# Dense experts of a small mixture layer: gating the outputs of plain tokens instead of gating the inputs

## The chip, the cores and the metric
The kernel runs on 1 core of one Trainium2 chip. The metric is the device time of one execution in microseconds (us), the median of several. All engines of the core take part: TensorE (PE, its weight loads shown as PEld), VectorE (DVE), ScalarE (ACT), GpSimd (POOL) and the DMA queues (SP, POOL).

## What is computed
Two layers over 4 batches of 1024 tokens with 128 features: a mamba mixer with an MLP, a first mixture of experts with residual and norms, attention with relative positions, and a second mixture with capacity. The change touches the first mixture alone:

```
gate_scores = softmax(x @ Wg.T + bg)
topk_scores, topk_idx = top_k(gate_scores, 2)
expert_outputs = einsum('bsd,eod->bseo', x, W) + b      # 8 experts, 128 -> 128
selected = take_along_axis(expert_outputs, topk_idx[..., None], axis=2)
output = sum(selected * topk_scores[..., None], axis=2)
```

All 8 experts are computed for all tokens; the gates of the 6 that were not chosen are zero.

## The kernel before, in words
Everything is float32 unless a line says bf16. A float32 product runs as two passes, so each matmul of the program is two matmul and two weight-load instructions in the trace.

**Slots.** The first layer is a pipeline over batches, written out by hand: `SLOTS` (L74) lists for each slot which batch is in the mixer (m), which in MLP and experts (p) and which in the tail, the norms, queries, keys and values before the attention (q). Slots 1, 2 and 3 have all of the work of the experts beside a mixer; slot 4 has (p = 3, q = 2) and no mixer; attention comes after slot 5. Each engine runs its own program in order, and they meet through semaphores.

**The loop over chunks.** In a slot the mixer goes through 8 chunks of 128 tokens, c = 0 to 7 (PE at L882, DVE at L2096, ACT at L1347). In each chunk PE does the product with the carried state (`chunk_carried`, L665), the new state (`chunk_state`, L657), transposes (`chunk_front`, L635), the decay sums (`chunk_after`, L650) and the output (`chunk_out`, L675). DVE does `chunk_carry` (L1884), `chunk_scaled` (L1901), `chunk_inputs` (L1875, L1878), `chunk_weights` (L1890, which waits for ACT's exponential, L1278), and after each second chunk `gate` (L1913, L1916). `chunk_out` of chunk c waits for `chunk_scaled` of c, and DVE's next chunk waits for PE's new state. At c = 7 PE runs `mix_out(m, 0)`; after the loop `mix_out(m, 1)`, which waits for the last `gate` and for ACT's squares (L1295). DVE closes the slot with `mix_norm` (L1930), two halves.

**The experts in that loop.** Tokens, turned so that features are on partitions, lie in `xnT` (128 x 1024). At c = 1 PE computes the logits (`route0`), at c = 2 and 3 DVE finds the two best and builds the gates `gsel` (128 tokens x 8 tiles x 8 experts). `gate_parts` (L1965) then cuts the gates into three bf16 parts `g3` (L1972 to L1977). At c = 4 PE turns `gsel` (8 transposes, L787) and `g3` (8 transposes, L791), ACT copies `gT` (L1262), DVE copies `g3T` (L1981). Then come 16 steps k, for each half H of the tokens and each expert e: `gate_rows` (L795) spreads the gate of expert e over 128 partitions by a bf16 product with `pick_rows`, DVE multiplies it with the tokens into `xs` (128x512, L1991), and `expert_sum` (L807) adds four 128x128 products with `w_exp` into one PSUM bank. Each half begins with the biases, four products of `gT` with `b_exp`, and ends with `expert_added` (L1993): one add into `x2` and the statistics of the norm (L1759, L1764). `SUMS_AT` and `SUMS_LAST` (L79) say at which chunk each step is issued: 0 to 2 at c = 4, 3 to 6 at c = 5, 7 to 10 at c = 6, 11 and 12 at c = 7, and 13 to 15 after `mix_out(m, 1)`. `keep_clock` (L596) issues bf16 products whose results nobody reads.

**Slot 4.** Without a mixer the steps are interleaved with the first products of attention: `score_pair` on PE and the maxima over them on DVE (`pair_max`, L2046), placed by `PAIRS_IN_SUMS` and `MAXIMA_IN_SUMS`.

Of the kernel before, what the change touches and what calls it, by code (L numbers as in the profile page):

```python
# [16 lines left out]
BF16 = mybir.dt.bfloat16  # L17
# [38 lines left out]
PAIRS_IN_SUMS = {1: 2, 3: 3, 5: 4, 8: 5, 11: 6, 13: 7}  # L56
MAXIMA_IN_SUMS = {0: 0, 1: 1, 3: 2, 5: 3, 7: 4, 11: 5, 13: 6, 15: 7}
# [10 lines left out]
XS_SLOTS = 4  # L68
# [10 lines left out]
SUMS_AT = {4: (0, 1, 2), 5: (3, 4, 5, 6), 6: (7, 8, 9, 10), 7: (11, 12)}  # L79
SUMS_LAST = (13, 14, 15)  # L80
# [32 lines left out]
def build(nc, t):  # L113

    with ExitStack() as ctx:
# [41 lines left out]
        b_exp = sb("b_exp", [E, D])  # L157
        pick_rows = sb("pick_rows", [3 * E, E, P], BF16)
# [153 lines left out]
        def sem(name):  # L312
# [34 lines left out]
        N_LATE = 5  # L347
# [63 lines left out]
        def col(ap):  # L411
# [14 lines left out]
            (w_exp[:], t["expert_wT"]), (b_exp[:], t["expert_b"]), (pick_in, t["pick_rows"]),  # L426
# [153 lines left out]
        def _(pe):  # L580
# [110 lines left out]
            def mix_out(b, H):  # L691
# [18 lines left out]
            def rows_turned_tail(b):  # L710
                for H in range(2):
# [3 lines left out]
                    else:  # L715
                        pe.wait_ge(S.xs_ready, 2 * E * (b + 1))
# [67 lines left out]
            def gates_turned(b):  # L784
                pe.wait_ge(S.gsel_ready, b + 1)
                for n in range(NT):
                    last = nc.tensor.transpose(bank((7, 5)[n // HT])[0:E, (n % HT) * P:(n % HT + 1) * P], gsel[:, n, :], ident[:])  # L787
                last.then_inc(S.gT_psum, 1)
                pe.wait_ge(S.g3_ready, 3 * b + 3)
                for n in range(NT):  # L790
                    last = nc.tensor.transpose(bank(6)[0:3 * E, :].bitcast(BF16)[:, n * P:(n + 1) * P],  # L791
# [1585 lines left out]
```

## Time and profile before
| | us |
|---|---|
| median of 3 runs (1543.93 to 1548.95) | 1547.5 |
| the profiled execution | 1547.93 |
| its span, first to last instruction | 1546.2 |
| PE busy | 1418.8 (92%) |
| DVE busy | 1075.2 (70%) |
| ACT busy | 863.1 (56%) |
| mean granted clock of TensorE | 0.952 |

The profiled execution takes 1.7 us more than its span. Slots 0 to 5 fill about the first 600 us, attention the stretch to about 1400 us, the second mixture and the last norm the rest. "Busy" counts an instruction from start to end; instructions of one engine overlap a little, so the cost of one in a row of like ones is the distance from start to start, not its duration. A granted clock of 1.00 is 2.4 GHz, 0.50 is 1.2 GHz.

### The profile page before, as it was taken

What the parts mean: (1) busy time and instruction counts of PE and PEld (TensorE: products, weight loads), DVE (VectorE), ACT (ScalarE), POOL (GpSimd) and SP (SyncE); (2) the same over time, 40 slices, a digit from 0 to 9 for tenths busy, and PEclk for the clock granted to TensorE, in tenths of its full rate; (3) what the DMA queues carried; (4) which work ended last, traced back from release to release, by engine and by line L of the source; (5) the groups of instructions that cost most, each with busy time, mean ns of one, the idle gap of its engine ahead of it and who ended that gap; (6) DMA issues with size and microseconds to landing.
All of it is one profiled execution on the core that took longest, in us unless ns stands there. A gap on an engine that the chain in (4) does not pass through costs nothing.

```text
span 1546.2 us, 21289 instructions
## 1 busy us (share of the span) xinstructions
PE 1418.8 (92%) x7543; PEld 635.6 (41%) x7543; DVE 1075.2 (70%) x2056; ACT 863.1 (56%) x1751; POOL 275.4 (18%) x409
## 2 busy tenths in 40 slices
PE   6998998899788988999999999999999999985786
PEld 3655665575556553222223232233322333322353
DVE  7766568738755577888887879888888888843023
ACT  6554235415531322677777777777777767773142
POOL 2211121102111203000000110501104111043452
PEclk9989899889979988999999999999999999998898
DMA  4080000200010922111101111011101100000135
GB/s 122 9 197 14 1 1 14 100 1 1 29 72 1 165 100 100 36 22 21 22 2 22 39 22 22 26 25 40 22 14 26 26 1 2 1 5 26 42 99 172
DMA packets 47343, 64.45 MB, mean 42 GB/s; under 512 B 9730, under 2 KB 34893, under 8 KB 45398
## 3 DMA queue, kind: packets, MB, share of 16 engines
q1 hardware_dynamic: 44166, 58.84, 14.9%
q0 software_dynamic: 3072, 4.25, 0.8%
q8 instruction: 61, 1.00, 0.3%
q14 instruction: 44, 0.36, 0.1%
HBM read 33.08 MB, written 32.03 MB: 42 GB/s over the span
## 4 chain that ended last, share of the span: by engine, by line
PE 59%; DVE 6%; ACT 2%; issue 2%; POOL 1%; DMA 1%; DVEq 0%; ACTq 0%; POOLq 0%
PE ps L591 57%; DVE smax L2046 2%; PE ps L584 1%; ACT space L1417 1%; POOL expert_in L1609 1%; DVE st L1759 1%; ACT space L1438 0%; PE ps L940 0%; DVE x_all L1777 0%; ACT space L1459 0%; PE ps L1072 0%; DMA shift_rows<-shiftT 0%; DMA space<-expert_in 0%; DVE x L1995 0%; DVE mv L1764 0%
## 5 line engine op out<-in xcount | busy, mean ns | idle before, releaser
L591 PE MATMUL ps<-space 128*32 128x512 f32 (+5 forms) x4608 | 846.7, 476 | 33.5 <-DVE space L1901 14.2
L2046 DVE TENSOR_REDUCE smax<-ps 128x1 f32<-128x1024 f32 x512 | 605.1, 1219 | 119.1 <-PE ps L591 113.0
L1417 ACT ACTIVATE space<-ps 128x512 f32<-128x512 f32 x1024 | 555.2, 595 | 211.1 <-PE ps L591 210.5
L591 PEld LDWEIGHTS ps<-space 128*32 128x32 f32 (+5 forms) x4608 | 248.6, 109 | 604.7 <-ACT space L1417 328.9
L1510 POOL TENSOR_SCALAR eps_sum<-mv 128x4 f32<-128x4 f32 x32 | 7.3, 229 | 615.1 <-DVEq L1766 614.6
L1272 ACT ACTIVATE btok<-ps 128x128 f32<-128x128 f32 x32 | 8.9, 277 | 148.4 <-PE ps L591 68.1
L591 PE MATMUL ps<-ones,ident 128*128 128x512 bf16 x271 | 73.1, 423 | 15.9 <-POOLq L1613 12.3
L591 PE MATMUL ps<-w_exp,space 128*128 128x128 f32 x512 | 81.5, 311 | 0.0
L591 PEld LDWEIGHTS ps<-w_exp,space 128*128 128x128 f32 x512 | 69.8, 213 | 16.1 <-issue 15.9
L1860 DVE SCALAR_TENSOR_TENSOR space<-space,conv_w 128x512 f32<-128x512 f32 x96 | 71.1, 750 | 2.3
L1609 POOL DMA_INDIRECT expert_in<-space,slot x64 | 62.9, 982 | 36.3 <-issue 19.3
L591 PE MATMUL ps<-space,w_in 128*128 128x512 f32 x96 | 58.4, 726 | 3.4 <-ACT space L1214 1.9
L1991 DVE TENSOR_TENSOR space<-xnT,ps 128x512 f32<-128x512 f32 x64 | 41.9, 683 | 25.2 <-PE ps L591 25.1
L2299 DVE TENSOR_TENSOR space<-space,ps 96x512 f32<-96x512 f32 x16 | 10.9, 684 | 66.4 <-ACT space L1446 66.4
L1539 POOL TENSOR_TENSOR space<-space,decay 128x256 f32<-128x256 f32 x28 | 17.1, 612 | 184.3 <-issue 137.5
L591 PEld LDWEIGHTS ps<-ones,ident 128*128 128x128 bf16 x271 | 28.4, 108 | 51.2 <-issue 17.7
L1890 DVE TENSOR_TENSOR space<-space,Gm 128x512 f32<-128x512 f32 x32 | 24.5, 766 | 27.9 <-ACT space L1278 27.9
L1295 ACT ACTIVATE space<-space 128x512 f32<-128x512 f32 x16 | 10.0, 625 | 59.2 <-DVE space L1916 59.2
L1512 POOL TENSOR_TENSOR rstd<-eps_sum,neg_half 128x4 f32<-128x4 f32 x40 | 41.5, 1037 | 3.3
L1289 ACT ACTIVATE aU<-upto,av 128x128 f32<-128x128 f32 x128 | 40.6, 395 | 0.0
L584 PE MATMUL ps<-ident,space 128*128 128x128 f32 x192 | 29.5, 286 | 12.0 <-DVE space L1827 11.3
L591 PE MATMUL ps<-xnT,w_gate 128*128 128x512 f32 x64 | 34.0, 613 | 5.6 <-DVE space L1949 4.8
(252 smaller groups left out, 1487.7 us busy)
## 6 DMA issues: line engine op xcount, KB each, us to landing
q_rows<-space SPq DMA_DIRECT2D x24, 256.0 KB, 2.4
k_rows<-space SPq DMA_DIRECT2D x24, 256.0 KB, 2.9
space<-k_rows SPq DMA_DIRECT2D x16, 384.0 KB, 5.3
space<-q_rows SPq DMA_DIRECT2D x16, 384.0 KB, 7.0
expert_out<-x_all SPq DMA_DIRECT2D x2, 2048.0 KB, 21.3
space<-expert_out SPq DMA_DIRECT2D x4, 1024.0 KB, 8.6
v_rows<-space SPq DMA_DIRECT2D x4, 668.0 KB, 3.6
space<-v_rows SPq DMA_DIRECT2D x4, 668.0 KB, 6.6
```

What stands on the lines that cost most here:

```text
L584: last = nc.tensor.transpose(tile(dst, i), src(i), ident[:])
L591: return nc.tensor.matmul(out, lhsT, rhs, start=first, stop=last)
L1289: last = nc.scalar.activation(aU[:, c % 2, h], upto[:], ACT.Copy, scale=av[:, c, h:h + 1])
L1417: nc.scalar.activation(prob[:, QUAD * (step % PROB_SETS) + unit % QUAD, :], bank(STB + unit % 2), ACT.Exp)\
L1512: g.tensor_tensor(out, eps_sum[:, 0:n], neg_half[:, 0:n], ALU.pow).then_inc(done, 1)
L1539: g.tensor_tensor(xw[:, c % 2], xdt[:, c % 2], decay[:, 0, c].unsqueeze(2).to_broadcast([P, SSM_HEADS, SSM_DIM]), ALU.mult).then_inc(S.xw_ ...
L1609: g.indirect_dma_start(expert_in, bass.IndirectOffsetOnAxis(ap=slot[:, k, i:i + 1], axis=0), xrow[:, i, k, :], None, bounds_check=E * CAPA ...
L1759: last = mine.mark(v.bn_stats(st[:, i, :], src[:, i, :]))
L1860: ins = v.scalar_tensor_tensor(out, raw[:, f, lo + k:lo + k + HALF], conv_w[:, f, k:k + 1], out, ALU.mult, ALU.add)
L1890: v.tensor_tensor(Wm[:, c % 2], EL[:, c % 2], Gm[:, c % 2].unsqueeze(1).to_broadcast([P, SSM_HEADS, P]), ALU.mult).then_inc(S.w_ready, 1)
L1991: v.tensor_tensor(xs[:, k % XS_SLOTS], xnT[:, half(H)], bank(6 + k % 2), ALU.mult).then_inc(S.xs_ready, 1)
L2046: v.tensor_reduce(smax[:, N % 2, i:i + 1], ps[:, b0:b0 + 2, :].rearrange("p k n -> p (k n)"), AX.X, ALU.max).then_inc(S.s_max, 1)
```

## The change
The experts' products take the plain tokens: the stationary operand is a tile of `xnT` (128 tokens), the moving one the weights of four experts side by side (128x512). The result has tokens on partitions and four experts in the columns of one bank, and VectorE applies the gate of each expert as a scalar per token while it adds from PSUM into `x2`. There are 8 pairs of such products per batch (two tiles of tokens, four experts), and each pair is followed on DVE by 8 instructions of 128x128 (two tiles, four experts); for one tile they form a chain through `x2`, and each waits for the one two places before it. The biases come from one transpose of all gates (128x64), one copy by ACT, and two products with a block table `b_exp` (64 x 1024, prepared on the host), added by `bias_added`. The cut of the gates into parts, their transposes, `gate_rows`, `xs`, `pick_rows` with its load and its copy by ACT, and in the slots with a mixer all `keep_clock` of the experts' part are gone.

```diff
-PAIRS_IN_SUMS = {1: 2, 3: 3, 5: 4, 8: 5, 11: 6, 13: 7}
-MAXIMA_IN_SUMS = {0: 0, 1: 1, 3: 2, 5: 3, 7: 4, 11: 5, 13: 6, 15: 7}
+PAIRS_IN_SUMS = {1: 2, 2: 3, 3: 4, 4: 5, 5: 6, 6: 7}
+MAXIMA_IN_SUMS = {0: (0, 1), 2: (2,), 3: (3,), 4: (4,), 5: (5,), 6: (6,), 7: (7,)}
-SUMS_AT = {4: (0, 1, 2), 5: (3, 4, 5, 6), 6: (7, 8, 9, 10), 7: (11, 12)}
-SUMS_LAST = (13, 14, 15)
+EXPERT_BANKS = (6, 7), (4, 5), (6, 7), (6, 7), (4, 5), (6, 7), (6, 7), (5, 6)
+PRODUCTS_AT = {2: (0,), 3: (1,), 4: (2,), 5: (3,), 6: (4, 5), 7: (6,)}
+SCALED_AT = {3: (0,), 4: (1, 2), 5: (3,), 6: (4, 5), 7: (6,)}
+BIAS_AT, LAST_PAIR = 5, 7
-        b_exp = sb("b_exp", [E, D])
-        pick_rows = sb("pick_rows", [3 * E, E, P], BF16)
+        b_exp = sb("b_exp", [NT * E, NT * D])
...
             def gates_turned(b):
                 pe.wait_ge(S.gsel_ready, b + 1)
-                for n in range(NT):
...
+                pe.wait_ge(S.experts_used, 2 * E * b + 4)
+                nc.tensor.transpose(bank(5)[0:NT * E, 0:P], gsel[:].rearrange("p t e -> p (t e)"), ident[:]).then_inc(S.gT_psum, 1)
+
+            def expert_biases(b):
+                pe.wait_ge(S.gT_sb, b + 1)
+                for H in range(2):
+                    mm(bank(4 + H), gT, b_exp[:, half(H)]).then_inc(S.bias_psum, 1)
+
+            def expert_pair(b, k):
+                if k == 0:
+                    pe.wait_ge(S.xnT_ready, turned("moe", b) + 2)
+                    pe.wait_ge(S.route_shift, 2 * b + 1)
+                elif k == 4:
+                    pe.wait_ge(S.moe_added, 2 * b + 2)
+                elif k >= 2:
+                    used = {2: 2, 3: 6, 5: 8, 6: 12, 7: 14}[k]
+                    pe.wait_ge(S.experts_used, 2 * E * b + used)
+                for w in range(2):
+                    mm(bank(EXPERT_BANKS[k][w]), tile(xnT, 2 * (k // 2) + w),
+                       w_exp[:, HT * (k % 2):HT * (k % 2) + HT, :].rearrange("p e d -> p (e d)")).then_inc(S.experts_psum, 1)
...
-                    if p is not None and c == HT:
-                        if m is None:
-                            keep_clock(OUTB, 16)
-                            score_pair(0)
-                            score_pair(1)
+                    if p is not None and c == BIAS_AT:
                         gates_turned(p)
-                        if m is not None:
-                            keep_clock(OUTB, 5)
                     if m is not None:
                         chunk_out(m, c)
...
-                        if c == HT:
-                            gate_rows(p, 0)
-                            gate_rows(p, 1)
-                        if m is not None and HT <= c < NT - 1:
-                            keep_clock(OUTB, 2)
-                        for k in SUMS_AT.get(c, ()):
-                            expert_sum(p, k)
+                        if c == 2 and m is None:
+                            keep_clock(YB, 10)
+                            score_pair(0)
+                            score_pair(1)
+                        if c == BIAS_AT:
+                            expert_biases(p)
+                        for k in PRODUCTS_AT.get(c, ()):
+                            if m is None and k == 1:
+                                keep_clock(5, 8)
+                            expert_pair(p, k)
                             if m is None and k in PAIRS_IN_SUMS:
                                 score_pair(PAIRS_IN_SUMS[k])
-                            if k == E - 1:
-                                keep_clock(OUTB, 3)
                 if m is not None:
                     mix_out(m, 1)
                 if p is not None:
+                    expert_pair(p, LAST_PAIR)
...
+            def bias_added(b):
+                dve.wait_ge(S.experts_used, 2 * E * b + 6)
+                for H in range(2):
+                    dve.wait_ge(S.bias_psum, 2 * b + H + 1)
+                    v.tensor_tensor(x2[:, own(H), :], x2[:, own(H), :], tiles4(4 + H), ALU.add).then_inc(S.moe_added, 1)
+
+            def experts_scaled(b, k):
+...
+                dve.wait_ge(S.experts_psum, 2 * E * b + 2 * k + 2)
+                earlier = {}
+                for e in range(HT):
+                    for w in range(2):
+                        i = 2 * (k // 2) + w
+                        if e:
+                            mine.wait(earlier[w])
+                        ins = v.scalar_tensor_tensor(x2[:, i, :], tiles4(EXPERT_BANKS[k][w])[:, e, :],
+                                                     gsel[:, i, HT * (k % 2) + e:HT * (k % 2) + e + 1], x2[:, i, :],
+                                                     ALU.mult, ALU.add)
+                        if e < HT - 1:
+                            earlier[w] = mine.mark(ins)
+                        else:
+                            ins.then_inc(S.experts_used, 1)
...
+                        if c == BIAS_AT:
+                            bias_added(p)
+                        for k in SCALED_AT.get(c, ()):
+                            experts_scaled(p, k)
+                            if k == LAST_PAIR // 2:
+                                expert_statistics(p, 0)
...
+                    experts_scaled(p, LAST_PAIR)
...
-                for H in range(2):
-                    last = nc.scalar.activation(gT[:, half(H)], bank((7, 5)[H])[0:E], ACT.Copy)
+                nc.scalar.activation(gT, bank(5)[0:NT * E, 0:P], ACT.Copy).then_inc(S.gT_sb, 1)
```

Not shown: the functions that are taken out (`gate_rows`, `expert_sum`, `evac_parts`, `expert_inputs`, `expert_added`, the cut in `gate_parts`), the waits at the head of `experts_scaled` (pair 0 for the norm and its transposes, pairs 3 and 4 for `moe_added`, the others for the pair before), and the maxima, which in slot 4 follow each pair. On ACT the copy of the gates moves from c = 4 to c = 5 (`BIAS_AT`). Pair 7 (`LAST_PAIR`) is issued after `mix_out(m, 1)` on PE and scaled after the loop on DVE, ahead of `mix_norm(m, 0)`. Waits elsewhere on `xs_ready` and `moe_added` become waits on `experts_used` (ACT's on `experts_psum`) of the same batch, and `mix_out(b, 0)` also waits until pair 4 of the batch in the experts has left banks 4 and 5.

## Rows read from the trace of the kernel before

**Rows 1.** The chain that ended last, slot 3: start us, us, what

```profile
450.97 11.62 PE ps L591 x42
```

**Rows 2.** Stretches of slots 1 to 4: us, busy of PE, PEld, DVE, ACT, POOL; PEclk, DMA

```profile
148.90:162.00 13.10, 10.29 (x67) 6.47 (x67) 9.86 (x51) 4.50 (x14) 2.37 (x4) 1.00 0.00 1
162.00:178.10 16.10, 14.26 (x60) 9.83 (x58) 4.71 (x11) 3.38 (x9) 1.18 (x2) 0.68 0.00 1
178.10:188.40 10.30, 9.99 (x64) 6.86 (x63) 6.06 (x12) 4.26 (x22) 3.09 (x4) 1.00 0.00 0
188.40:204.30 15.90, 14.87 (x104) 10.91 (x104) 6.86 (x19) 1.28 (x3) 0.00 (x0) 1.00 0.00 1
204.30:219.60 15.30, 13.92 (x109) 12.21 (x110) 10.19 (x29) 3.00 (x11) 5.67 (x8) 0.98 0.01 2
289.90:362.70 72.80, 67.52 (x394) 48.64 (x395) 37.70 (x120) 18.43 (x61) 12.20 (x18) 0.86 0.05 18
433.50:503.40 69.90, 60.20 (x372) 43.13 (x372) 36.59 (x118) 14.91 (x44) 9.72 (x16) 0.92 0.05 18
555.60:589.00 33.40, 32.37 (x202) 22.97 (x203) 24.82 (x47) 1.16 (x3) 1.26 (x2) 0.95 0.05 20
```

**Rows 3.** Timeline of PE: step starts at full clock (184 us), half clock (314 us)

```profile
184.57 0.39 PE L591 MATMUL ps<-space,pick_rows 24*128 24x512 bf16 x1
185.97 0.39 PE L591 MATMUL ps<-space,pick_rows 24*128 24x512 bf16 x1
...
314.19 0.60 PE L591 MATMUL ps<-space,pick_rows 24*128 24x512 bf16 x1
316.73 0.60 PE L591 MATMUL ps<-space,pick_rows 24*128 24x512 bf16 x1
```

**Rows 4.** Timeline of PE: passes of 128x512, a mixer chunk to the next, `mix_out` begins

```profile
265.58 3.17 PE L591 MATMUL ps<-xnT,w_qkv 128*128 128x512 f32 x7
268.58 1.61 PE L591 MATMUL ps<-w_qkv,xnT 128*128 128x128 f32 x13
...
51.81 0.60 PE L591 MATMUL ps<-hst,space 128*128 128x256 f32 x2
55.96 0.60 PE L591 MATMUL ps<-hst,space 128*128 128x256 f32 x2
...
200.57 0.68 PE L591 MATMUL ps<-w_out,space 128*128 128x128 f32 x4 [0.61 <-DVE space L1901]
```

**Rows 5.** DVE: scaled adds (min/median/max ns); timeline: scaled adds, dependent instructions, gated inputs

```profile
L1930 DVE SCALAR_TENSOR_TENSOR x<-ps,rstd_mix,xin x32: 339/343/351, 80.1 to 503.0; 128x128 f32<-128x128 f32 x32
...
213.82 1.12 DVE L1930 SCALAR_TENSOR_TENSOR x<-ps,rstd_mix,xin 128x128 f32<-128x128 f32 x4
222.25 1.58 DVE L1846 SCALAR_TENSOR_TENSOR dtp<-dtp,dts 128x32 f32<-128x32 f32 x7
180.95 1.92 DVE L1991 TENSOR_TENSOR space<-xnT,ps 128x512 f32<-128x512 f32 x3
```

**Rows 6.** Timeline of DVE: one chunk of the mixer without experts, and gate

```profile
52.06 0.87 DVE L1913 SCALAR_TENSOR_TENSOR space<-space,d_col,ps 128x256 f32<-128x256 f32 x2
53.58 0.41 DVE L1884 TENSOR_TENSOR hst<-hdec,ps 128x256 f32<-128x256 f32 x1
55.74 0.79 DVE L1890 TENSOR_TENSOR space<-space,Gm 128x512 f32<-128x512 f32 x1 [0.88 <-ACT space L1278]
```

**Rows 7.** The page, parts 5 and 6: the maxima; a load of 512 KB

```profile
L2046 DVE TENSOR_REDUCE smax<-ps 128x1 f32<-128x1024 f32 x512 | 605.1, 1219 | 119.1 <-PE ps L591 113.0
...
xin<-in_x SPq DMA_DIRECT2D x4, 512.0 KB, 4.2
```

**Rows 8.** PE's gaps and the clock: a timeline row, then stretches as in rows 2

```profile
133.29 0.94 PE L591 MATMUL ps<-space,btok 128*128 128x256 f32 x2 [2.40 <-POOL space L1539]
...
134.00:137.00 3.00, 3.00 (x10) 1.47 (x9) 1.38 (x4) 0.28 (x1) 1.35 (x3) 0.50 0.00 0
263.00:265.00 2.00, 0.00 (x0) 0.00 (x0) 0.62 (x2) 0.95 (x3) 1.92 (x4) 1.00 0.02 4
```

More of the change, by code:

```diff
@@ L425, in build @@
             (w_down[:], t["down_wT"].rearrange("(f p) d -> p f d", p=P)), (mlp_row[:], row(t["mlp_scale"])),
-            (w_exp[:], t["expert_wT"]), (b_exp[:], t["expert_b"]), (pick_in, t["pick_rows"]),
+            (w_exp[:], t["expert_wT"]), (b_exp[:], t["expert_b"]),
             (w_route0[:], t["route0_wT"]), (w_route1[:], t["route1_w"]), (b_route0[:], row(t["route0_b"])),
@@ L785, in gates_turned @@
                 pe.wait_ge(S.gsel_ready, b + 1)
-                for n in range(NT):
[L787 to L791, printed above, removed]
-                                               g3[:, n].rearrange("p s e -> p (s e)"), ident16[:])
@@ L1343, in _ @@
                     evac_queries(q)
-                if m == 0:
-                    act.wait_ge(S.w_late, LATE_LOADED)
-                    nc.scalar.activation(pick_rows[:].rearrange("k e n -> k (e n)"), pick_in, ACT.Copy).then_inc(S.late_ready, 1)
                 for c in range(NT):
@@ L1352, in _ @@
                         decays_so_far(m, c + 2)
-                    if p is not None and c == HT:
+                    if p is not None and c == BIAS_AT:
                         evac_gates(p)
@@ L2134, in _ @@
                 if p is not None:
-                    for k in SUMS_LAST:
-                        expert_step(p, k)
-                        if m is None and k in MAXIMA_IN_SUMS:
-                            pair_max(MAXIMA_IN_SUMS[k])
+                    experts_scaled(p, LAST_PAIR)
+                    if m is None:
+                        for pair in MAXIMA_IN_SUMS[LAST_PAIR]:
+                            pair_max(pair)
                 if m is not None:
@@ L2350 @@
     qkv_order = np.concatenate([by_dim, D + by_dim, 2 * D + np.arange(D)])
+    biases = np.zeros((NT, E, NT, D), np.float32)
+    for i in range(NT):
+        biases[i, :, i, :] = x["L0_ffn_b"]
     arrays = {
@@ L2358 @@
         "mixer_scale": x["L0_attn_mixer_scale"], "mlp_scale": x["L0_attn_mlp_scale"],
-        "expert_wT": x["L0_ffn_W"].transpose(2, 0, 1), "expert_b": x["L0_ffn_b"],
+        "expert_wT": x["L0_ffn_W"].transpose(2, 0, 1), "expert_b": biases.reshape(NT * E, NT * D),
         "route0_wT": x["L0_ffn_Wg"].T, "route0_b": x["L0_ffn_bg"],
@@ L2365 @@
         "route1_w": x["L1_ffn_w_gate"], "c_fc": x["L1_ffn_c_fc"], "c_proj": x["L1_ffn_c_proj"],
-        "pick_rows": np.repeat(np.tile(np.eye(E, dtype=np.float32), (3, 1)), P, axis=1),
         "pos_query": query, "pos_key": key,
```

97 lines of the change are left out of this document (22 added, 75 removed).

## The prediction
> **What bounds the kernel now.** I first read the chain that ended last. In slot 3, where the steps of the experts begin, it lies on PE without a break for 11.6 us from 451.0 [rows 1]; in slot 4 PE is busy for 32.4 of 33.4 us [rows 2]. So I cut the second half of the loop over chunks into stretches at DVE's `chunk_carry` [rows 2]. In slot 1, chunks 2 and 3 take 13.1 us, chunk 4 16.1, chunk 5 10.3, chunk 6 with `mix_out(m, 0)` 15.9, and the rest to the end of `mix_norm(m, 1)` 15.3, in all 70.7 us; the same in slots 2 and 3 is 72.8 and 69.9. From chunk 4 on PE is busy for 53.0 of 57.6 us, DVE for 27.8. Chunk 4 stands out: 14.3 us of PE, the granted clock 0.68, DVE busy only 4.7. A mixer chunk alone needs 4.15 us from one product with the state to the next [rows 4]. So PE's queue bounds this half of the loop, and the experts fill it.
>
> **What is removed from PE.** One of the 16 old steps costs 185.97 - 184.57 = 1.40 us at the full clock and 316.73 - 314.19 = 2.54 us at half [rows 3]: 22.4 us per batch at full clock. With them go the biases (16 passes of the step's kind, whose own eight are (1.40 - 0.3)/8 = 0.14 us each, so 2.2), 16 small transposes (the same again at most) and 14 clock-keeping products (each as the gate's row product, 0.3 at most): 27 to 31 us together.
>
> **What is added to PE.** A float32 pass of 128x512 costs (268.58 - 265.58)/7 = 0.43 us at the full clock [rows 4]. A pair is two products, four passes: 1.71 us; eight pairs 13.7 us, the biases four passes 1.7 us, one transpose 0.2 us: 15.6 us. PE gains 11 to 15 us per batch at the full clock. This is no saving yet, for DVE has to follow.
>
> **DVE.** The nearest row for a scaled add is `mix_norm`: the same operation, a 128x128 float32 source in PSUM, one in SBUF, a scalar per token. Four take 1.12 us at 0.343 each, so (1.12 - 0.343)/3 = 0.26 from start to start [rows 5]. The new ones wait for the one two places before. That one ended 0.52 - 0.34 = 0.18 us earlier; a dependent instruction starts about 0.03 us behind its predecessor's end (seven of 128x32 in 1.58 us, 0.23 apart at a duration of 0.19, [rows 5]). So I take 0.262, and 2.1 us for a pair; the other end, if a wait closes the overlap, is 0.34 + 0.03 = 0.38. Per batch: 64 x 0.262 = 16.8 us in, against 16 x 0.64 = 10.2 [rows 5] and the cut and the copy of the gates, out: five small instructions like those 0.23 apart, less one that overlaps, 0.9, and one as long as a gated input, 0.6. DVE gains 5 us of work per batch. The two adds of `expert_added` become the two of `bias_added`.
>
> **The sum in a slot with a mixer.** I laid both queues side by side with these prices. DVE's own chunk is 2.16 us from carry to `chunk_weights` (0.88 of it the wait for ACT) and 0.70 for that; `gate` takes 53.58 - 52.06 = 1.52 every second chunk [rows 6].
> - Chunks 2 and 3, 13.1 us: pair 0 comes in (+2.1), the cuts go (-0.9): 14.3.
> - Chunk 4, 16.1 us: DVE has 2.0 us of mixer (the exponential is ready when DVE is late) and pairs 1 and 2, whose products are ready: 6.3. PE has 4.15 + 1.7.
> - Chunk 5, 10.3 us: PE must do chunk 5's output, biases and pair 3, which end 5.7 us in; DVE adds the biases under that, then scales pair 3 (2.1), takes the statistics (1.4, the rest of the 4.0 below less the two `mix_norm`) and `gate` (1.5): 10.7.
> - Chunk 6 with `mix_out(m, 0)`, 15.9 us: output of chunk 6 at 2.3, pair 4 at 4.0, scaled to 6.2, pair 5 to 8.3, `chunk_scaled`, then `mix_out`, 204.3 - 200.6 = 3.7 us [rows 2, 4]: 12.3.
> - The rest, 15.3 us: here the new order costs. `gate` of the last two chunks stands on DVE behind pair 6, which waits for chunk 7's output and its own products: 3.3 + 2.1, gate 1.5, ACT's squares 0.7, `mix_out(m, 1)` 3.7, pair 7 1.7, its scaling 2.1. From the first `mix_norm` (213.8, [rows 5]) to the end at 219.6 it is 5.8 us now; the add of 0.7 and PE's 1.1 that it waited for go: 4.0. Together 19.1.
>
> That is 62.7 us instead of 70.7, a gain of 8.0; against the measured 72.8 and 69.9 it is 10.1 and 7.2; together 25.3. The head of the next slot hangs on the end of `mix_norm` as before.
>
> **The clock.** After a gap of 2.40 us on PE, 134 to 137 us ran at 0.50; after one of 2.0 us, 263 to 265, the clock stayed [rows 8]. The half-rate stretch of 3.3 us costs 1.7 us of work. My schedule has three such gaps: 3.2 us ahead of chunk 6's output, 2.6 ahead of `mix_out(m, 0)`, 4.3 ahead of `mix_out(m, 1)`, and the clock-keeping products are gone. I charge two drops per slot, 3.4 us, 10.2 in three slots (ends: 0 and 6 us per slot; the first is what the trace shows for a gap of 2.0 us, the second is three drops and a longer pair). The low clock in chunk 4 of before is already in the 16.1.
>
> **Slot 4.** The stretch takes 33.4 us with DVE busy 24.8 [rows 2]. Out go 16 x 0.68 and the 1.5, in come 16.8: 29.2 us of DVE in a row, and each maximum of 1.22 us [rows 7] lies between two pairs. Pairs 6 and 7 can only start once the pair before has left its banks: 1.7 - 1.2 = 0.5 us of wait each at the full clock, 2.2 at half. I take no change (ends -3 and +3).
>
> **The small edits.** `b_exp` grows from 4 to 256 KB, `pick_rows` (96 KB) goes: by the load of 512 KB in 4.2 us [rows 7] 1.3 us more on the queue, at zero, because nobody waits for the late weights in slot 0; uncovered it would cost those 1.3. ACT loses two copies and moves one from chunk 4 to 5, where PE's bias products wait for it; 0.3 us, inside chunk 5. The wait of `mix_out(m, 0)` for pair 4 is of the batch before: met long ago. No DMA is moved past a queue.
>
> **The sum.** 1547.93 for the profiled execution, less 25.3, plus 10.2: 1532.8. The execution lies 0.4 us above the median of the runs, so 1532.4; I give 1532.
>
> **Rivals.**
> - *Full clock throughout.* PE is busy above 80% in the shorter stretches, and in chunks 2 and 3 before it kept 1.00 at 10.3 of 13.1 us [rows 2]. Then the 10.2 us aren't paid and slot 4 gains 3: 1519. Against it: over chunk 4 of before the clock was 0.68 with PE busy 14.3 of 16.1 us [rows 2].
> - *The clock eats it.* Each gap drops the clock, the last one still when `mix_out(m, 1)` and pair 7 (together 5.4 us at full) run: 6 us per slot, 18 in all, and slot 4 gets 3 slower: 1547.5 - 25.3 + 18 + 3 = 1543, no change that can be told. For it: 0.50 after 2.40 us [rows 8]. The Trainium skill, "TensorE: Matmul & The Clock Gate", section "HAM oscillation", says that a loop whose waits are longer than its bursts starts each burst cold; here bursts between gaps are 4 to 9 us long, so it would make three cold starts per slot.
> - *DVE's step is 0.38, not 0.26* (the slower side). Its place is `experts_scaled`: if the waits inside it take away the overlap with the next instruction, a pair costs 3.0 us, 7.6 us more per batch, and as DVE then ends every stretch from chunk 3 on, nearly all of it counts: 4 x 7.6 = 30 us, 1532 + 30 = 1562. It turns the sign from (15.1 / 256) + 0.262 = 0.32 us per instruction. Against it: gated inputs with two waits each still overlap (three in 1.92 us at 0.68 each, [rows 5]). The Trainium skill, "VectorE: DVE Perf Modes", section "The DRAIN you can't avoid", says that the next operation does not start until the pipe is empty. By that rule a step would be the full 0.34 us and the time 1532 + 20 = 1552; rows 5 contradict it for instructions that are ready, and cannot show it for those with a wait on the one before last.
> - *The change doesn't do what it says*: the products of float32 with tokens on the stationary side are the same passes as before, so I see no way in which that fails and give it no share.
>
> **How the numbers follow.** The forecast's own family (the stretches shrink, some drops, 1524 to 1542) has 0.62, full clock 0.13, the clock eats it 0.13, DVE's step 0.12. The range takes in the full-clock case with 4 us of error of my schedule, 1515, and on the upper side the case of no change with as much, 1547; it leaves out the slow rival. About 0.3% (4.6 us) is what a measurement of this kernel can tell from no change. Faster gets the first two, 0.75; within 0.3% 0.13; slower 0.12.
>
> **What would show it.** In the changed profile: the matmul group of `w_exp` has 128x512 passes, 128 of them at about 0.43 us apart; 256 scaled adds, 0.26 apart in rows of eight; chunk 4's stretch near 6 to 8 us instead of 16; a wait of `mix_out(m, 1)` for `gate` that is longer than before; slot 4 within 3 us of 33.4. I am wrong if the adds are 0.32 apart or more, if chunk 5 or 6 takes over 3 us more than laid out, or if the granted clock over the same stretches of slots 2 and 3 is lower than the 0.86 and 0.92 of before [rows 2].

## The result and the profile after

The changed kernel takes 1590.3 us (median of 4 runs, 1588.8 to 1591.5) against 1547.1 for the kernel before on the same chip: ratio 1.0281, interval 1.0261 to 1.0301. It is slower by 43 us; forecast were 1532. The profiled execution is one of 1589.5 us.

The page of the changed kernel: span, busy time, granted clock in 40 slices, and three of its groups.

```profile
span 1587.7 us, 20197 instructions
PE 1411.2 (89%) x6944; PEld 604.7 (38%) x6944; DVE 1096.0 (69%) x2228; ACT 859.1 (54%) x1746; POOL 275.8 (17%) x409
...
PEclk9979869986987698899999999999999999998898
...
L1965 DVE SCALAR_TENSOR_TENSOR x<-ps,gsel,x 128x128 f32<-128x128 f32 x256 | 69.0, 342 | 73.4 <-PE ps L586 73.1
L586 PE MATMUL ps<-w_exp,xnT 128*128 128x512 f32 x128 | 84.5, 801 | 3.3 <-DVE x L1965 3.3
L586 PE MATMUL ps<-w_out,space 128*128 128x128 f32 x128 | 34.2, 415 | 25.2 <-ACT space L1266 16.1
```

DVE's 256 scaled adds take 342 ns each, as forecast. The 128 passes of the experts average 801 ns; their median is 595 ns, a pass at full clock, and the longest, at half clock, take 1222 ns, so about a third of the passes ran at half clock (an estimate from these three). In the clock's slices (39.7 us each) the later chunks of slots 1, 2 and 3 are slices 5 and 6, 9 and 10, 13 and 14: they read 8 and 6, 8 and 6, 7 and 6. The products with `w_out`, those of `mix_out`, have 25.2 us of idle time ahead of them.

Stretches of slot 1 (chunks 2 and 3, chunk 4, chunk 5, chunk 6 with `mix_out(m, 0)`, the rest, all), then all of slots 2 and 3, and slot 4; columns as in [rows 2]:

```profile
150.28:164.64 14.36, 11.34 (x55) 6.51 (x54) 11.22 (x56) 4.51 (x14) 2.37 (x4) 1.00 0.01 2
164.64:172.61 7.97, 7.08 (x28) 4.21 (x28) 6.21 (x23) 2.44 (x7) 1.18 (x2) 0.79 0.00 0
172.61:188.54 15.93, 11.24 (x33) 5.10 (x31) 8.33 (x28) 4.42 (x23) 3.10 (x4) 0.79 0.00 1
188.54:205.99 17.45, 13.66 (x56) 10.23 (x58) 6.62 (x23) 1.28 (x3) 0.00 (x0) 0.72 0.00 0
205.99:232.27 26.28, 17.47 (x62) 12.40 (x63) 10.63 (x39) 2.87 (x11) 5.08 (x8) 0.63 0.00 1
150.28:232.27 81.99, 60.78 (x230) 38.45 (x230) 43.01 (x163) 15.52 (x58) 11.73 (x18) 0.76 0.00 1
304.64:386.05 81.41, 60.90 (x229) 37.49 (x230) 42.92 (x163) 17.41 (x60) 11.98 (x18) 0.76 0.04 16
458.67:542.47 83.80, 61.92 (x219) 37.65 (x219) 41.70 (x161) 14.11 (x42) 9.46 (x16) 0.71 0.04 15
594.70:628.00 33.30, 23.28 (x55) 8.31 (x53) 27.68 (x82) 0.36 (x2) 1.27 (x2) 0.90 0.06 25
```

Slot 1 takes 82.0 us instead of 70.7, slot 2 81.4 instead of 72.8, slot 3 83.8 instead of 69.9 [rows 2]: 34.0 us. Between these stretches lie another 5.2 us (1.4 ahead of slot 1; 72.4 and 72.6 from slot to slot instead of 70.3 and 70.9), and about 1 us in slot 4 (from the gates to the last add to `x`: 33.2 us, 32.1 before). That makes 40 of the 41.5 us between the two profiled executions. By the prediction's prices PE's work in a slot is 11 to 15 us less at the full clock, yet its busy time in slot 1 is still 60.8 us: the clock over the slot went from 0.92 to 0.76.

The timeline of PE in slot 1; in brackets the idle time ahead and what ended it:

```profile
165.53 0.62 PE L586 MATMUL ps<-space 128*64 128x128 f32 x4 [3.15 <-DVE space L1869]
...
176.10 3.78 PE L586 MATMUL ps<-b_exp,space 64*128 64x512 f32 x4 [0.95 <-ACT space L1234]
...
189.43 0.63 PE L586 MATMUL ps<-space 128*64 128x128 f32 x4 [3.94 <-DVE space L1869]
...
199.37 0.82 PE L586 MATMUL ps<-w_out,space 128*128 128x128 f32 x4 [2.90 <-DVE space L1869]
...
215.66 1.20 PE L586 MATMUL ps<-w_out,space 128*128 128x128 f32 x4 [4.54 <-ACT space L1266]
...
222.48 3.76 PE L586 MATMUL ps<-w_exp,xnT 128*128 128x512 f32 x4
```

The granted clock in stretches of that timeline:

```profile
176.00:180.00 4.00, 3.90 (x5) 1.36 (x6) 0.78 (x2) 2.38 (x17) 1.39 (x2) 0.50 0.01 4
199.40:205.00 5.60, 5.60 (x28) 5.60 (x29) 0.00 (x0) 0.00 (x0) 0.00 (x0) 0.53 0.00 0
205.00:209.00 4.00, 4.00 (x19) 2.89 (x19) 1.46 (x3) 0.00 (x0) 2.37 (x4) 0.50 0.01 2
215.70:220.00 4.30, 4.30 (x20) 4.30 (x21) 0.00 (x0) 0.00 (x0) 0.00 (x0) 0.50 0.00 0
220.00:226.00 6.00, 6.00 (x18) 3.86 (x17) 0.00 (x0) 0.00 (x0) 0.00 (x0) 0.50 0.01 3
```

Behind the gaps of 3.15 and 3.94 us the chunk's output and the first part of what follows run at half clock, behind those of 2.90 and 4.54 us `mix_out`: its four products with `w_out` last 1.20 us instead of 0.68 [rows 4], and pair 7 lasts 3.76 instead of the 1.7 forecast. A fifth stretch at half clock begins with the biases, 3.78 us instead of the 1.98 that they take in e7, although the gap ahead of them is only 0.95 us (with one of 0.69 us, 2.6 us earlier). The low clock outlasts one step: from 215.7 to 226.0 it is 0.50 throughout.

DVE beside it:

```profile
211.22 2.16 DVE L1965 SCALAR_TENSOR_TENSOR x<-ps,gsel,x 128x128 f32<-128x128 f32 x8 [3.51 <-PE ps L586]
...
226.35 2.16 DVE L1965 SCALAR_TENSOR_TENSOR x<-ps,gsel,x 128x128 f32<-128x128 f32 x8 [11.45 <-PE ps L586]
```

DVE's rows of eight take 2.16 us, so (2.16 - 0.342)/7 = 0.26 us per step. It stands idle 11.45 us for pair 7, because pair 7 is queued on PE behind `mix_out(m, 1)`, which waits for `gate`, which waits on DVE behind the scaling of pair 6.

### The profile page after: what moved, and what is told of

Read it like the earlier page. It is cut to its first block, busy times and chain, and to the rows that moved or that the text cites. A ratio compares the mean times of both kernels' runs of the same rounds, so it can differ in the third digit from the quotient of the medians.

```text
span 1587.7 us, 20197 instructions
## 1 busy us (share of the span) xinstructions
PE 1411.2 (89%) x6944; PEld 604.7 (38%) x6944; DVE 1096.0 (69%) x2228; ACT 859.1 (54%) x1746; POOL 275.8 (17%) x409
## 4 chain that ended last, share of the span: by engine, by line
PE 57%; DVE 7%; ACT 2%; issue 2%; POOL 1%; DMA 0%; DVEq 0%; POOLq 0%; ACTq 0%
PE ps L586 55%; DVE smax L2019 3%; DVE x L1965 2%; PE ps L579 1%; ACT space L1385 1%; POOL expert_in L1577 1%; DVE st L1727 1%; ACT space L1406 0%; PE ps L913 0%; DVE x_all L1745 0%; ACT space L1427 0%; PE ps L1045 0%; DVE mv L1732 0%; DMA space<-expert_in 0%; DMA expert_in<-space,slot 0%
## 5 line engine op out<-in xcount | busy, mean ns | idle before, releaser
L586 PE MATMUL ps<-space 128*32 128x512 f32 (+5 forms) x4608 | 850.9, 478 | 57.4 <-DVE space L1869 31.7
L1965 DVE SCALAR_TENSOR_TENSOR x<-ps,gsel,x 128x128 f32<-128x128 f32 x256 | 69.0, 342 | 73.4 <-PE ps L586 73.1
L586 PE MATMUL ps<-w_exp,xnT 128*128 128x512 f32 x128 | 84.5, 801 | 3.3 <-DVE x L1965 3.3
L586 PE MATMUL ps<-ones,ident 128*128 128x512 bf16 x228 | 61.0, 429 | 18.5 <-POOLq L1581 12.3
L586 PE MATMUL ps<-w_out,space 128*128 128x128 f32 x128 | 34.2, 415 | 25.2 <-ACT space L1266 16.1
L586 PEld LDWEIGHTS ps<-ones,ident 128*128 128x128 bf16 x228 | 24.5, 109 | 52.6 <-issue 21.0
L586 PEld LDWEIGHTS ps<-w_exp,xnT 128*128 128x128 f32 x128 | 30.6, 259 | 35.9 <-issue 30.0
L1480 POOL TENSOR_TENSOR rstd<-eps_sum,neg_half 128x4 f32<-128x4 f32 x40 | 41.5, 1038 | 3.3
```

Of the source, the lines that this page charges most:

```text
L586: return nc.tensor.matmul(out, lhsT, rhs, start=first, stop=last)
L1480: g.tensor_tensor(out, eps_sum[:, 0:n], neg_half[:, 0:n], ALU.pow).then_inc(done, 1)
L1965: ins = v.scalar_tensor_tensor(x2[:, i, :], tiles4(EXPERT_BANKS[k][w])[:, e, :], gsel[:, i, HT * (k % 2) + e:HT * (k % 2) + e + 1], x2[:, ...
```

## The experiments

Theory A: the new order leaves gaps on PE in which the clock drops, and half-rate products cost more than the removed work saves. Theory B: the order of the waits alone costs it, whatever the clock does. Theory C: the 256 scaled adds are too much for DVE. (In the expectations the letters behind A belong to each run: "rival C" of e3 is not theory C.) The kernels below ran on two other chips, e1 to e7 and r_after on one, e8 to e10 on the other; on both the kernel before takes 1591 to 1592 us. Times written in absolute us in the expectations of e1 to e4 are for the first chip and miss by these 44 us, so ratios and stretches decide. Slot 1 in each, from the same view as above (us):

| | c. 2, 3 | c. 4 | c. 5 | c. 6, out 0 | rest | sum | clock |
|---|---|---|---|---|---|---|---|
| before | 13.1 | 16.0 | 10.3 | 15.9 | 15.3 | 70.7 | 0.92 |
| as laid out in the prediction | 14.3 | 6.3 | 10.7 | 12.3 | 19.1 | 62.7 | - |
| changed | 14.4 | 8.0 | 15.9 | 17.5 | 26.3 | 82.0 | 0.76 |
| e1: fillers in four gaps | 14.4 | 7.1 | 14.4 | 13.0 | 19.4 | 68.2 | 0.97 |
| e5: filler in the last gap | 15.1 | 9.3 | 15.2 | 15.7 | 21.5 | 76.6 | 0.83 |
| e8: biases later | 14.4 | 8.0 | 9.4 | 17.4 | 26.4 | 75.5 | 0.79 |
| e7: biases later, fillers | 14.4 | 7.1 | 9.4 | 13.6 | 19.4 | 63.8 | 1.00 |
| e9: new order | 14.4 | 7.1 | 9.4 | 12.7 | 10.6 | 54.1 | 1.00 |

**e1_fill: the gaps filled.** Products of `ones` with `ident` that nobody reads, into a bank whose reader is done: 8 ahead of chunk 4's output, 13 ahead of chunk 6's, 10 ahead of `mix_out(m, 0)`, 17 ahead of `mix_out(m, 1)`.

```diff
+            def filled(b, used, at, n):
+                if n:
+                    pe.wait_ge(S.experts_used, 2 * E * b + used)
+                    keep_clock(at, n)
...
+                    if p is not None:
+                        filled(p, 10, 5, 17)
                     mix_out(m, 1)
```

> The changed kernel with unread bf16 products put into four gaps of PE in the slots with a mixer (8 ahead of chunk 4's output, 13 ahead of chunk 6's, 10 ahead of the first mix_out, 17 ahead of the second). Theory A (the gaps drop the clock and half-rate products are what is lost): the granted clock over the second half of the three loops rises from about 0.6 to above 0.85, a stretch that took 82 us takes 63 to 70, and the kernel takes 1535 to 1560 us instead of 1590. Rival B (the two queues wait for each other and the clock is only a companion): the stretches stay within 4 us of 82 and the kernel stays above 1580.

Measured: 1597.1 us against 1591.3, ratio 1.0059 (1.0027 to 1.0092). Chunk 5, chunk 6, the rest and the whole of slot 1; then PE's biases and pair 3, and the last filler with what follows it:

```profile
171.89:186.25 14.36, 12.44 (x44) 5.70 (x44) 8.33 (x28) 4.42 (x23) 3.09 (x4) 0.88 0.01 1
186.25:199.29 13.04, 11.59 (x66) 7.42 (x68) 6.61 (x23) 1.28 (x3) 0.00 (x0) 1.00 0.00 0
199.29:218.64 19.35, 13.73 (x79) 8.74 (x80) 10.64 (x39) 2.87 (x11) 5.07 (x8) 0.98 0.00 1
150.40:218.64 68.24, 56.75 (x278) 32.45 (x278) 43.01 (x163) 15.51 (x58) 11.71 (x18) 0.97 0.00 1
```

```profile
175.38 2.46 PE L586 MATMUL ps<-b_exp,space 64*128 64x512 f32 x4 [0.95 <-ACT space L1247]
177.77 3.15 PE L586 MATMUL ps<-w_exp,xnT 128*128 128x512 f32 x4
...
202.38 3.83 PE L586 MATMUL ps<-ones,ident 128*128 128x512 bf16 x17
207.09 0.68 PE L586 MATMUL ps<-w_out,space 128*128 128x128 f32 x4 [0.87 <-DVE space L1897]
```

PE has more to do and slot 1 is 13.8 us shorter than with the change alone, at 0.97; the first product of `mix_out(m, 1)` is back at 0.68 us. So the clock is the larger part of the loss, shown by adding work. Chunk 5 stays at 14.4 us. Even so the kernel is no faster than before. Its three slots sum to 5.6 us less than those of before, but 2.5 us come back between slots 1 and 2 (72.8 us for 70.3) and 3.7 between slots 2 and 3 (74.6 for 70.9), so that the last `mix_norm` ends 2.0 us later than in before. The ratio stands for 9 us, the medians for 5.8; where what is left of it lies is open, since the profiled execution is the shortest of the five (1588.7 us) and the kernel before has no profile on this chip.

**e2_nokeep: the kernel before without its clock-keeping products beside the experts' steps.**

```diff
                         gates_turned(p)
-                        if m is not None:
-                            keep_clock(OUTB, 5)
...
-                        if m is not None and HT <= c < NT - 1:
-                            keep_clock(OUTB, 2)
...
-                            if k == E - 1:
+                            if k == E - 1 and m is None:
                                 keep_clock(OUTB, 3)
```

> The kernel before without the unread products of the experts' part in slots with a mixer (5, then 3 times 2, then 3 in each of three slots). Theory A expects that the old order, in which PE has work without a break, loses little: its drop in chunk 4 is there already; 1545 to 1560 us. If the unread products themselves were what held the old kernel up, it comes to 1575 or more, near the changed kernel.

Measured: ratio 1.0033 (1.0006 to 1.0059), 3 to 5 us. Chunk 6 of slot 1:

```profile
190.03:213.45 23.42, 21.31 (x99) 16.84 (x98) 6.87 (x19) 1.28 (x3) 0.00 (x0) 0.64 0.00 1
```

Here chunk 6 takes 23.4 us at 0.64 instead of 15.9 at 1.00 [rows 2], and slot 1 loses 9.9 us in all; slots 2 and 3 lose 3.6 and 0.9 us. The profiled execution, 1600.0 us, is 5 us above the median of its ten runs. These 14 products per slot were worth something, but they are not what the change lost: without them the old order is still 35 us per execution better than the changed one.

**e3_fewer: 64 scaled adds instead of 256.** The outputs of three of four experts are left out of the sum.

```diff
-                for e in range(HT):
+                for e in (HT - 1,):
...
-                        if e:
+                        if e < HT - 1:
                             mine.wait(earlier[w])
```

> The changed kernel with one of four scaled adds: VectorE adds only the last expert of each group of four, 64 adds instead of 256; the other experts' outputs are left out of the result. The products on PE are the same. Theory A with VectorE's adds as what opens the gaps expects PE's waits ahead of the chunk outputs to shrink below 2 us and the clock to hold in most of the stretch: 1515 to 1550 us. Rival C (the new place of gate and squares behind pair 6 and the bias at chunk 5 open the gaps whatever the adds cost) expects 1570 or more.

Measured: ratio 0.9878 (0.9852 to 0.9904). The last stretch and the whole of slot 1:

```profile
189.90:210.73 20.83, 14.64 (x64) 10.83 (x64) 7.45 (x27) 2.87 (x11) 5.33 (x8) 0.75 0.00 1
148.15:210.73 62.58, 50.26 (x232) 32.05 (x231) 30.62 (x115) 15.52 (x58) 11.96 (x18) 0.89 0.00 1
```

With 12.6 us less on DVE per batch (48 x 0.262) slot 1 is 19.4 us shorter than with the change. DVE's adds take part, but more goes than they cost, at a clock of 0.89 instead of 0.76: that they set how long PE stands still fits this, and the gap ahead of chunk 6's output is 2.39 us here instead of 3.94. The last gap is still there (2.99 us), and the last stretch, at 0.75, still 5.5 us above that of before. That all 256 adds are not too much for DVE (theory C) is shown by e9 below, which keeps them and needs 54.1 us for slot 1.

**e4_order: the queues in the order of what is ready.** On PE pairs 1 to 4 go ahead of the chunk's output, pair 6 ahead of `mix_out(m, 0)` and pair 7 ahead of `mix_out(m, 1)`; DVE adds the biases behind pair 3 and scales pair 6 ahead of `mix_variance(m, 0)`.

```diff
+PAIRS_FIRST = {3: (1,), 4: (2,), 5: (3,), 6: (4,)}
+PAIRS_AFTER = {2: (0,), 6: (5,), 7: (7,)}
...
+                        elif p is not None:
...
+                            expert_pair(p, 6)
+                            mix_out(m, 0)
...
+                        for k in PAIRS_FIRST.get(c, ()):
+                            expert_pair(p, k)
                     if m is not None:
                         chunk_out(m, c)
...
+                        if p is not None:
+                            experts_scaled(p, 6, True)
                         mix_variance(m, 0)
```

> The changed kernel with another order in the slots with a mixer: pairs 1 to 4 ahead of the chunk's output on PE, pair 6 ahead of the first mix_out and pair 7 ahead of the second, the biases added behind pair 3, pair 6 scaled ahead of the variance. No unread products are added. Theory A expects fewer and shorter gaps, the wait ahead of the second mix_out down from 4.5 us to about 2, and 1550 to 1575 us. Rival B expects about the same gain from the order alone as from fillers, at an unchanged clock.

Measured: 1550.8 us, ratio 0.9763 (0.9736 to 0.9791); slots 1 to 3 at 57.4, 55.5 and 55.7 us. The gain over the kernel before is 40 us, beyond what either theory expected; the prediction gave the change 15. Against the changed kernel (r_after, next) it is 80 us, and 78.5 of them lie in the three slots.

**r_after: the changed kernel on this chip.**

> The changed kernel itself, on the chip of the three runs beside it, for the earlier ones ran on a chip where the kernel before takes 44 us more than in the first runs, and attention after the experts is the part that is longer there. Theory (PE's gaps drop the clock, and only slots 1 to 3 are worse): the changed kernel is 36 to 45 us slower than the kernel before here too, ratio 1.023 to 1.029; the five stretches of slots 1, 2 and 3 come to 82, 81 and 84 us against 71, 73 and 70. Rival (the loss is worth less where the clock drops in attention anyway, because what follows makes up for it): ratio under 1.015.

Measured: 1630.5 us, ratio 1.0236 (1.0201 to 1.0272); the three slots 81.8, 81.4 and 83.8 us, the same as on the first chip to 0.2 us. The first maximum of attention starts at 596.8 us on the first chip and at 596.5 here: up to there the chip makes no difference. What follows is longer. From the first maximum to the last it is 838.4 us instead of 812.3, at a mean clock of 0.97 instead of 0.99; from the last maximum to the end, with the second mixture in it, 194.4 instead of 178.6, at 0.86 instead of 0.91. Together these are 41.9 us. The middle of attention, 700 to 1400 us of the span, first chip and second:

```profile
700.00:1400.00 700.00, 698.03 (x3959) 212.13 (x3961) 589.94 (x760) 517.38 (x961) 81.82 (x131) 1.00 0.10 20
```

```profile
700.00:1400.00 700.00, 679.82 (x3816) 205.68 (x3809) 566.59 (x714) 498.24 (x925) 81.19 (x130) 0.98 0.10 20
```

On this chip e1's fillers take 33.4 us off the changed kernel (1597.1 against 1630.5), most of its 38 us of loss.

**e5_last_gap: a filler in the last gap alone** (the counts of e1 are 0, 0, 0 and 17).

> The changed kernel with 17 unread products ahead of mix_out(m, 1) alone; the other three gaps stay open. Theory A1 (each gap prices itself: the half clock covers only the work behind the gap): the last stretch falls from 26.3 to about 19.4 us as with all four fillers, chunks 4 to 6 keep their 8.0, 15.9 and 17.4 us in slot 1; the sum of slot 1 is about 75, and the kernel is 18 to 24 us faster than the changed one. Rival A2 (once the first gap has dropped the clock, it stays down for the rest of the slot, and a filler at the end comes too late): the last stretch stays above 24 us and the kernel is within 8 us of the changed one. Rival A3 (filling the last gap also brings back chunk 6 of the next slot): more than 30 us faster.

Measured: ratio 1.0117 (1.0081 to 1.0153), 18.7 us under the changed kernel of the same job. Chunk 6 and the last stretch of slot 1:

```profile
189.57:205.25 15.68, 11.89 (x56) 9.15 (x58) 6.62 (x23) 1.28 (x3) 0.00 (x0) 0.82 0.00 0
205.25:226.73 21.48, 15.86 (x81) 9.85 (x81) 10.63 (x39) 2.87 (x11) 5.08 (x8) 0.89 0.00 1
```

A1 holds: chunks 4 to 6 are as slow as before and the last stretch falls to 21.5, 2.1 us longer than e1's because it begins at the half clock that the gap ahead of `mix_out(m, 0)` left. So the last gap alone is worth 4.8 us per slot in place, more than the 3.4 us that were charged for all.

**e7_bias and e8_bias_only: the biases taken off pair 3's path**, with e1's fillers and without. Pair 3 goes ahead of chunk 5's output on PE, and its scaling ahead of the biases' add on DVE.

```diff
+                    if p is not None and m is not None and c == BIAS_AT:
+                        expert_pair(p, 3)
                     if m is not None:
                         chunk_out(m, c)
...
-                            experts_scaled(p, k)
+                            experts_scaled(p, k, m is not None)
+                            if k == LAST_PAIR // 2 and m is not None:
+                                bias_added(p, 8)
...
```

> The changed kernel with all four fillers, and beside them one part of the order alone: pair 3 goes ahead of chunk 5's output on PE, and DVE adds the biases behind the scaling of pair 3 instead of ahead of it. With the fillers alone chunk 5 took 14.4 us in slot 1 where 10.7 were laid out. Theory B (the path transpose of the gates, ACT's copy, bias products, DVE's add stands ahead of pair 3 and is what chunk 5 waits for): chunk 5 falls to 11 to 12 us, the sum of slot 1 from 68.2 to about 65, and the kernel is 6 to 10 us faster than with the fillers alone, so below the kernel before, ratio 0.998 to 1.001. Rival (chunk 5's output on PE is what it waits for, and the biases come for nothing inside that): chunk 5 stays above 13.5 us and the ratio stays near 1.006.

> The changed kernel without any filler, with one part of the order alone: pair 3 ahead of chunk 5's output on PE, the biases added behind the scaling of pair 3. With all four fillers beside it this took the sum of slot 1 to 63.8 us at a clock of 1.00; here the gaps ahead of chunk 6's output, mix_out(m, 0) and mix_out(m, 1) stay open. Theory A (gaps that remain keep dropping the clock): chunks 6 and the rest stay at about 16 to 17.5 and 26 us as in the changed kernel, chunk 5 falls from 15.3 or 15.9 to 10 to 12 us, and the kernel is 12 to 18 us under the changed one: ratio to the kernel before 1.012 to 1.017. Rival (moving pair 3 alone takes away what started the drops): clock of slot 1 over 0.90 and ratio under 1.005.

Measured: e7 1580.2 us, ratio 0.9920 (0.9886 to 0.9954); e8 1614.3, ratio 1.0149 (1.0121 to 1.0177). Chunk 5, chunk 6 and the rest of slot 1, of e7 with the whole slot, then of e8:

```profile
171.66:181.04 9.38, 9.25 (x38) 4.68 (x39) 8.15 (x27) 4.41 (x23) 3.09 (x4) 1.00 0.01 2
181.04:194.62 13.58, 13.02 (x73) 7.87 (x73) 6.62 (x23) 1.28 (x3) 0.00 (x0) 1.00 0.00 1
194.62:213.97 19.35, 13.73 (x81) 8.75 (x81) 10.55 (x39) 2.87 (x11) 5.32 (x8) 1.00 0.00 1
150.18:213.97 63.79, 54.98 (x280) 31.88 (x279) 42.74 (x163) 15.51 (x58) 11.96 (x18) 1.00 0.00 1
```

```profile
171.28:180.67 9.39, 8.09 (x33) 3.90 (x31) 8.15 (x27) 4.43 (x23) 3.10 (x4) 1.00 0.01 2
180.67:198.03 17.36, 13.57 (x56) 10.16 (x58) 6.62 (x23) 1.28 (x3) 0.00 (x0) 0.73 0.00 0
198.03:224.41 26.38, 17.61 (x62) 12.48 (x63) 10.55 (x39) 2.88 (x11) 5.32 (x8) 0.63 0.00 1
```

Chunk 5 falls to 9.4 us in both, further than expected, and e7's ratio lies below the 0.998 to 1.001 expected. In e1 the biases began at 175.38 after 0.95 us of waiting for ACT's copy, lasted 2.46 instead of 1.98 us, and only then came pair 3, which was scaled 9.1 us into the chunk; now it is scaled 2.9 us in. Without the fillers the two later stretches stay at 17.4 and 26.4 us, as theory A said: the two parts are apart, 13.8 and 6.5 us taken alone (82.0 less 68.2 and 75.5), and 18.2 together. With both, slot 1 is at 63.8 us, near the 62.7 laid out (slots 2 and 3: 68.8 and 63.8).

**e6_order_fill, e9_order_again, e10_order_fill_again: the new order with and without fillers** (10 and 8 products, ahead of pair 6 and of `mix_out(m, 1)`).

> The kernel with the new order of pairs and chunk outputs, plus 10 unread products ahead of pair 6 and 8 ahead of mix_out(m, 1), in the two gaps that the order had left (1.83 and 2.48 us). Theory A: pair 6 behind the second gap took 3.68 us instead of 1.71, so the filler gives 1.5 to 2 us per slot back where it stays inside the gap, and the sum of a slot falls from 57 to about 55; time 3 to 6 us under that of the order alone, ratio to the kernel before 0.972 to 0.976. Rival (the fillers themselves stand in PE's queue when the scaling is done and cost as much as they give): within 3 us of the order alone, 0.976 to 0.979.

> The new order of pairs and chunk outputs without fillers, once more, beside the same with fillers, for the two were 0.0024 apart in ratio, in different jobs. If the order alone holds what it showed: ratio 0.974 to 0.979, the sum of a slot 55 to 57 us.

> The new order with 10 and 8 unread products in its last two gaps. Theory: the fillers give 1 to 2 us per slot (chunk 6 12.7 instead of 14.4 us), so 2 to 6 us less than the order alone. Rival: chunks 2 and 3 of slots 2 and 3 run at 0.80 instead of 1.00 and take it back, and the two are within 2 us.

Measured: with fillers 0.9739 (0.9683 to 0.9794), then 0.9725 (0.9701 to 0.9749); without, beside the latter, 0.9755 (0.9729 to 0.9781). The medians of the common job are 1548.6 and 1549.6 us. The last two stretches of slot 1 in e9, the two gaps on PE that the order leaves, and chunks 2 and 3 of slot 2 in e10:

```profile
181.48:194.14 12.66, 9.69 (x57) 6.52 (x58) 8.69 (x32) 1.28 (x3) 0.00 (x0) 1.00 0.00 1
194.14:204.71 10.57, 9.02 (x66) 7.04 (x67) 8.58 (x31) 2.99 (x11) 5.68 (x8) 1.00 0.01 2
```

```profile
172.23 1.98 PE L588 MATMUL ps<-w_exp,xnT 128*128 128x512 f32 x4 [1.83 <-DVE x L1981]
...
188.65 1.98 PE L588 MATMUL ps<-w_exp,xnT 128*128 128x512 f32 x4 [2.48 <-DVE x L1981]
```

```profile
278.21:295.61 17.40, 15.76 (x57) 8.72 (x58) 11.22 (x55) 6.39 (x16) 2.37 (x4) 0.80 0.18 70
```

The order alone takes slot 1 to 54.1 us at 1.00, and its gaps are 1.83 and 2.48 us; here neither dropped the clock. e7 has the full clock in slot 1 too and takes 63.8 us. So 9.7 us of slot 1 come from the order of the waits at an unchanged clock, 8.8 of them in the last stretch (19.4 to 10.6), where pair 6 is now scaled before it can hold up `gate` and pair 7 no longer follows `mix_out(m, 1)`: theory B holds for this part. e7's last fillers don't account for it, since PE still stands idle 0.87 us behind them. With the fillers chunk 6 is 12.7 us in all slots, but chunks 2 and 3 of slots 2 and 3 take 17.4 us in that execution, at 0.80, where they take 14.4 at full clock. The same 17.4 us stand in slot 3 of e9, without fillers, so the fillers need not be their cause. The three slots sum to 168.5 and 168.7 us without fillers (e4, e9) and to 174.8 and 175.5 with them (e6, e10), against the expectation, yet the medians of the whole kernel are 1 us apart the other way. The intervals overlap: whether the fillers help is left open. That the order beats both kernels was measured four times, twice with fillers.

## Why the prediction was wrong

**What bounds the kernel** held: PE's queue sets the slots, and slot 4, for which no change within 3 us was forecast, became 1.1 us longer.

**PE's work and DVE's step** held. At full clock a pair takes 1.88 to 1.98 us from first start to last end, 1.7 to 1.9 from start to start, against 1.71; the adds are 0.26 us apart, so the rival of 0.38 fell. [Rows 5] carried over to instructions that wait for the one before last. The Trainium skill's rule in "VectorE: DVE Perf Modes", section "The DRAIN you can't avoid", would have made rows of eight 8 x 0.342 = 2.7 us; they took 2.16. The same section says that a next operation that is not held starts earlier, which the prediction left out, and the trace agrees with that exception.

**The schedule in a slot** was right where the clock was full. With e1's fillers four of the five stretches are within 0.9 us of the layout (the rest: 19.1 laid out, 19.4 measured). The 0.8 us of chunk 4 are a misreading: I had the exponential ready when DVE comes for it, and DVE waits 0.88 us for it there as in [rows 6]. The miss is chunk 5: "output, biases and pair 3 end 5.7 us in" was 9.0 us in e1. I had left out that chunk 5's output waits for DVE behind the scaling of pair 2 (1.37 us of idle PE), that the biases wait 0.95 us for ACT, and that the clock was at 0.88 there. That is 3.7 us per slot beside the fillers, and e8 shows it as 6.5 us in the changed kernel.

**The clock** is the step that failed, and two of the prediction's own signs say so: chunks 5 and 6 of slot 1 took 5.2 us more than laid out each, and the clock over slots 2 and 3 was 0.76 and 0.71, under the 0.86 and 0.92 of before. I named the three gaps of the later chunks and charged "two drops per slot, 3.4 us", with 6 as the upper end, by one half-rate stretch of 3.3 us of before. The fillers gave 13.8 us back in slot 1, where 3.4 were charged. The gaps were longer than laid out, 3.94, 2.90 and 4.54 us for 3.2, 2.6 and 4.3, a fourth of 3.15 us lay ahead of chunk 4's output, the clock was also down in the biases and pair 3 behind gaps of only 0.69 and 0.95 us, and behind the last one the half clock lasted over 10 us, in which `mix_out(m, 1)` and pair 7 ran at twice their price. DVE waits for exactly these, so that stretch is on the path. That a late pair also lengthens the next gap, so that a drop costs more than its own products, I only argue from the order of the waits.

"The clock eats it" was the right mechanism of the rivals with too small a price: 18 us in three slots, where e1 against the changed kernel shows 13.8, 11.6 and 14.2, together 39.6. The rule of the Trainium skill in "TensorE: Matmul & The Clock Gate", section "HAM oscillation", that a loop whose waits outlast its bursts starts each burst cold, does not give the three cold starts that I drew from it, since the bursts laid out were longer than the waits. The trace shows half clock behind five gaps of slot 1, and there too the bursts were longer (7.0 us of products from 189.43, then 2.90 of gap): the rule's condition was not met and the cold starts came all the same.

**"The head of the next slot hangs on the end of `mix_norm` as before"** was wrong by about 2 us per slot. In the changed kernel PE starts it behind a gap of 4.28 us, and cold:

```profile
231.87 3.57 PE L586 MATMUL ps<-w_in,space 128*128 128x4 f32 x16 [4.28 <-ACT space L1158]
```

In the kernel before and in the new order the gap there is 0.80 us (with e1's fillers it is still 4.75, which is why time comes back there between the slots):

```profile
217.72 2.49 PE L591 MATMUL ps<-w_in,space 128*128 128x4 f32 x16 [0.80 <-ACT space L1185]
...
203.58 1.95 PE L588 MATMUL ps<-w_in,space 128*128 128x4 f32 x16 [0.80 <-ACT space L1174]
```

**The sum.** Forecast were 198.3 us for the three stretches of five (213.4 less 25.3 plus 10.2); they took 247.2. Of these 48.9 us more, 29.4 are the clock's (39.6 that the fillers give back, less the 10.2 charged), and 19.5 stay with the fillers in, 12.3 of them in chunk 5. The 48.9 us, 5.2 between the slots and 1 in slot 4 are 55 of the 56.7 us by which the profiled execution missed.

## What to carry to other kernels

When work is taken out of the engine that bounds, lay out where it will stand still afterwards, and if a gap of TensorE drops the clock, charge it with all that runs behind it at half rate up to the next full stretch, not with one short drop. The length of a single gap did not tell here whether it would: the clock fell behind 0.95 us and stayed up behind 2.99 (last section). In an in-order queue ask of every entry whether its input is ready when its turn comes: here the order alone (what is ready first, what DVE waits for next) turned +2.4% into -2.4%, with the same products and the same adds. Unread products in the gaps are a cheap test of whether a loss is the clock's.

## What the runs showed of the hardware

- In e9 a gap of 2.48 us ahead of pair 6 stands in each of the three slots. In slots 1 and 3 the pair behind it took 1.98 us, in slot 2 3.67 us at half clock (chunk 6: 12.7 against 14.3 us). The gap of 1.83 us ahead of pair 3 did the same: the pair took 1.98, 1.99 and 3.68 us in e9, 2.60, 3.68 and 3.68 in e10. e4 and e9, the same kernel on two chips, had slots of 57.4, 55.5, 55.7 and 54.1, 55.8, 58.9 us: a drop is not certain, and one trace can't tell what such a gap costs.
- In the changed kernel the biases and pair 3 ran largely at half clock behind gaps of 0.58 to 0.69 and 0.95 us in all three slots (0.53, 0.57 and 0.60 over 6 to 7 us). In slot 3 the gap of 2.99 us ahead of chunk 6's output left the clock at 1.00 for the 5.0 us behind it.
- On the second chip attention ran at 0.98 instead of 1.00, as shown with r_after, and in 700 us it got through about 4% fewer matmuls, 3816 records for 3959; what follows attention was slower too. The kernel before is 44 us slower there; no profile of it was taken on that chip, so that these are the same parts is inferred from the changed kernel alone.
- Fillers in the experts' slots did not raise the time by what they add: 48 products, 11.0 us of PE in slot 1, and slot 1 became 13.8 us shorter.
